# A graph network on one core: unbounded gathers in the second propagation, and three groups' scatters moved from the degrees to the node run

## The chip, the cores and the metric

The kernel runs on one core of a Trainium2 chip. The metric is the device time of one execution in microseconds (us). TensorE is called PE here, VectorE DVE, ScalarE ACT, GpSimd POOL and SyncE SP. A name with q behind it (SPq, ACTq, POOLq) is that engine's sequencer, which issues the DMAs.

## The reference

Four graph layers, each with a residual, work on 100000 nodes of 64 features and 50000 edges `(src, dst)`, which are sorted by `dst`. Only the first matters here. It is a Chebyshev convolution of order 3 with an attention layer behind it:

```python
h = jnp.maximum(_layernorm(x, axis=-1), 0.0)
...
deg = jax.ops.segment_sum(edge_attr, src, num_segments=n)
dinv = jnp.where(deg > 0, 1.0 / jnp.sqrt(jnp.where(deg > 0, deg, 1.0)), 0.0)
w = -(dinv[src] * edge_attr * dinv[dst])

def prop(h):
    return jax.ops.segment_sum(w[:, None] * h[src], dst, num_segments=n)
Tx1 = prop(Tx0)
...
Tx2 = 2.0 * prop(Tx1) - Tx0
```

`Tx1` of a node that is the `dst` of no edge is zero. The edges whose `src` is such a node therefore contribute nothing to the second `prop`.

## The kernel before

The edges lie in 49 groups of 1024 (8 slots of 128 partitions; `EP` = 50176 with padding), the nodes in 98 groups of 1024. The program is a row of stages, each a function with one block of code for each engine; a barrier stands between two stages. Inside a stage each engine runs a software pipeline of its own over the groups (`ring_loop`: every part of a group's work has a lag in steps and a place inside the step), and semaphores tie the engines together. The stages around the change:

- **Degrees** (`degrees`, 0 to 461 us). PE adds up the nodes' degrees as products of one-hot matrices; ACT and DVE build these. At the end DVE makes the factors `dinv` and SP stores them. Beside that POOL writes each edge's place into a table `d_pos` by its final id: one indirect DMA for 128 edges, eight for a group (`scatter_places`, L948). The first `PLACED_EARLY` = 40 groups are done here (L730, 320 DMAs), and POOL then waits for their landing (L731).
- **Node run** (`lone_nodes`, 461 to 1172 us). All 98 node groups are normalized and taken through the layer as if they had no edge. POOL scatters the other nine groups' places (L990, 72 DMAs), waits until all 16 columns of `d_xt` are written, and gathers the destination rows of the 49 edge groups (`gather_kept`, L1173, 8 indirect DMAs a group, 8 buffers). ACT issues these 16 column copies (L1110), one in each of its first 16 steps; every element is a packet of 4 bytes. SP's order is written out step by step: in step `s` it loads `x` of group `s` (L1002); loads the tails `d_dinv` and `d_pos` of group `s - TAIL_LATE` (L1008, L1009; the first of them waits for all scatters); stores the rows `d_ext` of group `s - EXT_LATE`, five steps later (L1013); stores `d_h` and `d_x` of group `s - 7` (L1018, L1022); and stores the gathered rows of edge group `e` at step `xd_turn(e)` (L1027). ACT writes the body of an `ext` row (L1127) early and its tail (L1132) at the lag of the tails, into a ring of 24 buffers.

```python
late = [[] for _ in range(TAIL_LATE - 2)]
ring_loop(act, NODE_GROUPS, [begin, columns], [scale], [base, tables], [mean], *late, [tails], lead=EXT_RING + 2,
          ring=EXT_RING)
```

- **First propagation** (1172 to 1703 us). For each edge group SP loads the source ids `near` and the group's `d_xd`, POOL gathers the source rows of `d_ext` (`gather_rows`, L1165, 8 indirect DMAs, 66 columns), DVE weighs them (`p_msg`, L1265), PE transposes them, DVE adds up along the edges (`run_sums`, a scan), and SP stores the running sums to `d_sums1`. From the last two columns of the gathered row DVE also makes `ls`, the row at which the source's sums lie: below `EP` where that node has incoming edges, at `EP` or beyond where it has none. A test `beyond` (L1260) on `ls` gives `ls2`. SP stores `ls` and `ls2`.
- **Second propagation** (1703 to 2256 us). SP loads `ls` as ids, and POOL gathers rows of `d_sums1` (65 columns) with a bound of `EP - 1`: an id beyond it moves nothing. What is not moved has to be zero already, so DVE clears each buffer `got` behind its use (L1406) and POOL waits for that. DVE weighs the rows (`p_msg`, L1402), PE transposes them (L1437), DVE scans, PE multiplies (L1446, L411, L1457), and so on.

The rest of the program (2256 to 5535 us) isn't touched.

Of the kernel before, what the change touches and what calls it, by code (L numbers as in the profile page):

```python
# [31 lines left out]
P = 128  # L32
# [25 lines left out]
HOT_RING = 16  # L58
HOT_PARTS = ((0, 96), (96, 96), (192, 64), (256, 64), (320, 72))
PRODUCT_PARTS = ((0, 208), (208, 64), (272, 120))  # L60
PLACED_EARLY = 40
PLACED_LATE = GROUPS - PLACED_EARLY
COLUMN_PARTS = 16
WIDE = 2 * S
NODE_RING = 8
H_LATE, X1_LATE = 7, 7
TAIL_LATE = 18
EXT_LATE = TAIL_LATE + 5
EXT_RING = 24


def xd_turn(e):

    return 22 + 17 * (e + 1) // 10


def of_slot(r, n):
# [304 lines left out]
def group_rows(a):  # L382
    return a.rearrange("(g p s) c -> g p s c", p=P, s=S)
# [74 lines left out]
def build(nc, A, out):  # L458
    ctx = ExitStack()
    with ctx:  # L460
# [14 lines left out]
        D = Bufs()  # L475
        D.hs = dram("d_hs", (EP, C))
        D.xt, D.xd = dram("d_xt", (NP_, C + 1)), dram("d_xd", (EP, C + 1))
        D.sums1 = dram("d_sums1", (EP, C + 1))
        D.h, D.x1 = (dram("d_" + name, (EP + NP_, C)) for name in ("h", "x1"))
        D.x23 = dram("d_x23", (2 * EP + NP_, C))  # L480
        D.hd, D.x1d, D.x2d, D.x3d = D.h[0:EP], D.x1[0:EP], D.x23[0:EP], D.x23[EP + NP_:2 * EP + NP_]
        D.h_lone, D.x1_lone, D.x2_lone = (a[EP:EP + NP_] for a in (D.h, D.x1, D.x23))
        D.ext = dram("d_ext", (NP_, C + 2))
        D.dinv, D.pos = dram("d_dinv", (NP_, 1)), dram("d_pos", (NP_, 1))
        D.ls, D.ls2 = (dram("d_" + name, (GROUPS, P, S), I32) for name in ("ls", "ls2"))
# [692 lines left out]
def first_propagation(nc, A, sem, W, D, bank):  # L1178

    ctx = ExitStack()  # L1180
    with ctx:
# [4 lines left out]
        near, ls, ls2 = (t("p1_" + n, [P, RING, S], I32) for n in ("near", "ls", "ls2"))  # L1186
# [4 lines left out]
        pd = t("p1_pd", [C, RING, G_ROWS])  # L1191
        norm = NormTwice(sem, t, "p1_n", bank(6))
        names = ("msg_done", "yd_done", "msg_t", "yd_t", "yf_done", "pd_mm", "back", "evacuated", "carry", "weighed",
                 "placed", "beyond", "wd_done", "placed2")
        m = {n: sem("p1_" + n) for n in names}
        inn, x_in, landed, st, ls_st = ([sem(f"p1_{n}{r}") for r in range(RING)] for n in (
            "in", "x_in", "got", "st", "ls_st"))
        with nc.Block() as block:
            @block.sync
            def _(sp):  # L1200
                for r in range(RING):
                    sp.sem_inc(st[r], 32)
                    sp.sem_inc(ls_st[r], 32)

                def load(i, r, g):
                    sp.wait_ge(m["msg_done"], g + 1)
                    sp.dma_start(near[:, r], A["src_rows"][g]).then_inc(inn[r], 16)
                    sp.wait_ge(m["yd_done"], g + 1)
                    sp.dma_start(xd[:, r], group_rows(D.xd)[g]).then_inc(x_in[r], 16)

                def store_places(i, r, g):
                    sp.wait_ge(m["placed2"], g + 1)
                    sp.dma_start(D.ls[g], ls[:, r]).then_inc(ls_st[r], 16)
                    sp.dma_start(D.ls2[g], ls2[:, r]).then_inc(ls_st[r], 16)

                def store(i, r, g):
                    sp.wait_ge(m["evacuated"], g * 2 + 2)
                    sp.dma_start(group_cols(D.pd)[g], pd[:, r]).then_inc(st[r], 16)
                    sp.dma_start(group_rows(D.sums1)[g], g1[:, r]).then_inc(st[r], 16)
                ring_loop(sp, GROUPS, [load], [], [store_places], [], [store])  # L1220
                for r in range(RING):
                    sp.wait_ge(st[r], 32 * (of_slot(r, GROUPS) + 1))
                    sp.wait_ge(ls_st[r], 32 * (of_slot(r, GROUPS) + 1))

            @block.gpsimd
            def _(pool):
                def gather(i, r, g):
                    hold(pool, inn[r], i * 16 + 16)
                    gather_rows(nc, pool, D.ext, near[:, r], got[:, r], landed[r])
                ring_loop(pool, GROUPS, [gather])  # L1230

            @block.vector
            def _(dve):
                dve.sem_inc(m["yd_done"], RING)
                dve.sem_inc(m["msg_done"], RING)
                nc.vector.memset(sums[:, 1, G_ROWS - 1:G_ROWS], 0.0).then_inc(m["carry"], 1)

                def a(i, r, g):
                    dve.wait_ge(x_in[r], i * 16 + 16)
                    yield from norm.centre(nc, dve, g, xd[:, r, :, 0:C])  # L1240
                    yield 3
                    nc.vector.scalar_tensor_tensor(out=wd[:, r % 2], in0=xd[:, r, :, C], scalar=-1.0, in1=of_group(W.ewE, g),
                                                   op0=ALU.mult, op1=ALU.mult).then_inc(m["wd_done"], 1)
                    yield from norm.scale(nc, dve, g)
                    if not (isinstance(g, int) and g == 0):
                        dve.wait_ge(m["yd_t"], g)
                    nc.vector.tensor_tensor(yd[:], norm.y, spread(norm.gain), ALU.mult).then_inc(m["yd_done"], 1)

                def messages(i, r, g):
                    yield 3  # L1250
                    w = of_group(W.wE, g)
                    dve.wait_ge(landed[r], i * 128 + 128)
                    dve.wait_ge(ls_st[r], i * 32 + 32)
                    dve.wait_ge(m["wd_done"], g + 1)
                    nc.vector.tensor_tensor(w, got[:, r, :, C], wd[:, r % 2], ALU.mult).then_inc(m["weighed"], 1)
                    nc.vector.tensor_tensor(ls[:, r], got[:, r, :, C + 1], of_group(W.loneE, g), ALU.min
                                            ).then_inc(m["placed"], 1)
                    yield 6
                    dve.wait_ge(m["placed"], g + 1)
                    nc.vector.tensor_scalar(beyond[:], ls[:, r], EP, EP + NP_, ALU.is_lt, ALU.mult).then_inc(m["beyond"], 1)  # L1260
                    dve.wait_ge(m["weighed"], g + 1)
                    if not (isinstance(g, int) and g == 0):
                        dve.wait_ge(m["msg_t"], g)
                    nc.vector.tensor_scalar(msg[:, :, C], w, 1.0, None, ALU.mult)
                    nc.vector.tensor_tensor(msg[:, :, 0:C], got[:, r, :, 0:C], spread(w), ALU.mult).then_inc(m["msg_done"], 1)  # L1265
                    dve.wait_ge(m["beyond"], g + 1)
                    nc.vector.tensor_tensor(ls2[:, r], ls[:, r], beyond[:], ALU.add).then_inc(m["placed2"], 1)

                def scan(i, r, g):
                    yield 4  # L1270
                    dve.wait_ge(m["msg_t"], g + 1)
                    if not (isinstance(g, int) and g < 2):
                        dve.wait_ge(m["back"], g - 1)
                    dve.wait_ge(m["carry"], g + 1)
                    run_sums(nc, W, g, r % 2, bank(4, 2)[0:C + 1], sums, m)
                ring_loop(dve, GROUPS, [a, messages], [scan])
# [65 lines left out]
def second_propagation(nc, A, sem, W, D, bank):  # L1342

    ctx = ExitStack()
    with ctx:
# [7 lines left out]
        names = ("msg_done", "zeroed", "msg_t", "carry", "mm", "pre_done", "slanted", "h_done", "back", "att_mm", "evacuated",  # L1353
                 "pd_in0", "pd_in1")
        m = {n: sem("p2_" + n) for n in names}
        pd_in = (m["pd_in0"], m["pd_in1"])
# [1 line left out]
        with nc.Block() as block:  # L1358
            @block.sync
            def _(sp):  # L1360
# [2 lines left out]

                def load(i, r, g):
                    sp.wait_ge(m["msg_done"], g + 1)
                    sp.dma_start(near[:, r], D.ls[g]).then_inc(inn[r], 16)

                def load_later(i, r, g):
                    sp.wait_ge(m["pre_done"], g + 1)
# [10 lines left out]
            @block.gpsimd  # L1380
            def _(pool):
                def gather(i, r, g):
                    hold(pool, inn[r], i * 16 + 16)
                    hold(pool, m["zeroed"], g + 1)
                    gather_rows(nc, pool, D.sums1, near[:, r], got[:, r], landed[r], EP - 1)
                ring_loop(pool, GROUPS, [gather])

            @block.vector
            def _(dve):
                dve.sem_inc(m["msg_done"], RING)  # L1390
                dve.sem_inc(m["pre_done"], 2)
                for r in range(RING):
                    nc.vector.memset(got[:, r], 0.0).then_inc(m["zeroed"], 1)
                nc.vector.memset(sums[:, 1, G_ROWS - 1:G_ROWS], 0.0).then_inc(m["carry"], 1)

                def messages(i, r, g):
                    yield 4
                    dve.wait_ge(landed[r], i * 128 + 128)
                    if not (isinstance(g, int) and g < 2):
                        dve.wait_ge(m["msg_t"], g - 1)  # L1400
                    w = W.wE[:, bass.ds(g, 1)].rearrange("p a s -> p (a s)")
                    nc.vector.tensor_tensor(msg[:, r % 2], got[:, r], spread(w, C + 1), ALU.mult  # L1402
                                            ).then_inc(m["msg_done"], 1)
# [1210 lines left out]
```

## Time and profile before

| | |
|---|---|
| median of 3 runs | 5541.77 us (5536.04 to 5545.48) |
| the profiled execution | 5537.43 us, its span 5535.3 us |
| busy share of the span: PE, DVE, ACT, POOL | 64%, 73%, 50%, 66% |
| mean granted clock of TensorE | 0.78 |
| mean DMA traffic | 108 GB/s |

No engine is busy all the time: each stage has its own limit, so the shares over the whole span tell little. The rows further down are cut by stage. Times in them are counted from the span's start. "Issue" as the end of an idle time means that the engine waited for nothing that the profile shows; the 0.30 us between two of POOL's indirect DMAs are of that kind.

### The profile page before, as it was taken

The numbers are of one execution on the slowest core, as the hardware profiler recorded it, in microseconds if no ns is written. First come the engines' busy times: TensorE is split into PE (matmuls) and PEld (weight loads), VectorE is DVE, ScalarE is ACT, GpSimd is POOL, SyncE is SP. The second block draws the span as 40 slices with busy tenths as digits, with TensorE's granted clock in tenths as the row PEclk, the third lists the DMA queues.
The fourth block names the chain that finished last, engine by engine and source line by source line (L and its number), as shares of the span: only waits on it lengthen the run. The fifth ranks groups of instructions, "written<-read, shape, count | busy, mean of one in ns | idle before, by whom it ended". The sixth has DMA issues, their size and how long they took to land. (4 is left out here: it accounts for less than half of the span.)

```text
span 5535.3 us, 72269 instructions
## 1 busy us (share of the span) xinstructions
PE 3564.5 (64%) x15275; PEld 1835.2 (33%) x15275; DVE 4044.6 (73%) x6567; ACT 2757.9 (50%) x6379; POOL 3627.5 (66%) x3647
## 2 busy tenths in 40 slices
PE   8992788847776999677728867777455545661110
PEld 5551555523332333244414433333222212221000
DVE  8873698857774555699869969999555569996442
ACT  6662677733331222476629966666322247772221
POOL 7777277757775777577713347665377767765777
PEclk9996999978785555699959989999666668885555
DMA  8549977754442222466514433333344423322221
GB/s 99 74 62 43 109 232 232 230 146 108 103 108 55 62 62 62 134 212 195 183 60 138 135 98 84 84 84 84 91 129 132 125 68 77 77 68 67 70 74 48
DMA packets 535690, 595.56 MB, mean 108 GB/s; under 512 B 297571, under 2 KB 312041, under 8 KB 533948
## 3 DMA queue, kind: packets, MB, share of 16 engines
q1 hardware_dynamic: 319036, 473.91, 29.2%
q0 software_dynamic: 112896, 91.81, 9.2%
q10 hardware_dynamic: 103648, 28.71, 6.6%
q8 instruction: 29, 0.48, 0.0%
q14 instruction: 81, 0.66, 0.0%
HBM read 354.69 MB, written 303.31 MB: 119 GB/s over the span
## 5 line engine op out<-in xcount | busy, mean ns | idle before, releaser
L1165 POOL DMA_INDIRECT l_got<-d_x,l_near x1176 | 1139.2, 969 | 562.1 <-issue 373.7
L1173 POOL DMA_INDIRECT ln_xd<-d_xt,idsE x392 | 370.1, 944 | 208.3 <-issue 119.2
L2480 POOL DMA_INDIRECT out<-fi_res,fi_near x392 | 381.1, 972 | 181.0 <-issue 118.5
L1165 POOL DMA_INDIRECT p_got<-d_sums,p_near x392 | 399.5, 1019 | 151.7 <-issue 150.5
L948 POOL DMA_INDIRECT d_pos<-placeE,finE x392 | 401.9, 1025 | 146.4 <-issue 135.6
L1165 POOL DMA_INDIRECT p_got<-d_h,p_near x392 | 384.8, 982 | 156.5 <-issue 117.2
L1165 POOL DMA_INDIRECT p_got<-d_ext,p_near x392 | 378.5, 965 | 162.8 <-issue 117.1
L892 PE MATMUL ps<-hot_lo,hot_w 128*128 128x392 bf16 x2352 | 391.9, 330 | 15.6 <-ACT hot_w L930 15.6
L930 ACT ACTIVATE hot_w<-hot_hi,vals 128x128 bf16<-128x128 bf16 x784 | 267.9, 393 | 126.2 <-DVE hot_lo L787 114.5
L411 PE MATMUL ps<-ident,fi_sums 64*128 64x64 f32 x392 | 53.1, 314 | 424.8 <-DVE fi_sums L1338 424.8
L1338 DVE TENSOR_TENSOR_SCAN p_sums<-same,p_sums,ps 65x1024 f32<-65x1024 f32 (+1 forms) x98 | 229.5, 2342 | 95.1 <-PE ps L1437 90.9
L892 PEld LDWEIGHTS ps<-hot_lo,hot_w 128*128 128x128 bf16 x2352 | 230.3, 98 | 176.8 <-issue 17.7
L404 PE MATMUL ps<-ident,l_hn 128*128 128x128 f32 x588 | 111.2, 321 | 230.8 <-DVE l_hn L2259 205.2
L418 PE MATMUL ps<-l_df,l3ab 128*64 128x512 f32 x196 | 165.4, 998 | 128.4 <-DVE l_neg L2380 128.4
L1338 DVE TENSOR_TENSOR_SCAN l_sums<-same,l_sums,ps 64x1024 f32<-64x1024 f32 (+1 forms) x98 | 228.7, 2334 | 5.7
L2568 ACT ACTIVATE ps<-fi_hh,fi_sc 64x1024 f32<-64x1024 f32 x49 | 59.0, 1205 | 336.8 <-DMA fi_hh<-d_hh 332.6
L1468 ACT ACTIVATE p_slant<-ps 64x1024 f32<-64x1024 f32 x49 | 49.8, 1017 | 348.6 <-DVE ps L1420 348.6
L1988 PE MATMUL ps<-at_pf,gatw 128*64 128x512 f32 x392 | 178.2, 597 | 54.3 <-DVE at_sums L1338 53.9
L1912 POOL TENSOR_TENSOR at_wide<-at_wide,at_own 128x512 f32<-128x512 f32 x49 | 70.3, 1434 | 215.9 <-DVE at_wide L1932 214.7
L2547 DVE TENSOR_TENSOR fi_res<-fi_xd,ps 128x512 f32<-128x512 f32 x49 | 33.6, 685 | 241.9 <-POOLq L2487 241.9
L418 PE MATMUL ps<-l_hf,l2w 128*64 128x512 f32 x196 | 173.5, 1041 | 46.5 <-ACT l_hf L2303 46.5
L240 ACT ACTIVATE l_hn<-l_s_xc,l_s_rstd 128x64 f32<-128x64 f32 x784 | 196.3, 333 | 0.3 <-DVE l_s_rstd L226 0.3
(388 smaller groups left out, 10934.3 us busy)
## 6 DMA issues: line engine op xcount, KB each, us to landing
l_xd<-d_x SPq DMA_DIRECT2D x147, 256.0 KB
d_ext<-ln_ext SPq DMA_DIRECT2D x98, 264.0 KB, 2.2
d_xt<-in_x_wide ACTq DMA_DIRECT2D x49, 520.0 KB
ln_x<-in_x SPq DMA_DIRECT2D x98, 256.0 KB
d_h<-ln_hb SPq DMA_DIRECT2D x98, 256.0 KB, 3.0
d_x<-ln_x SPq DMA_DIRECT2D x98, 256.0 KB
lb_x<-d_x SPq DMA_DIRECT2D x49, 512.0 KB
d_x<-lb_x SPq DMA_DIRECT2D x49, 512.0 KB
```

The lines of the kernel that those rows point to most:

```text
L240: last = nc.scalar.activation(out[:, n], self.xc[:, r % 2, n], func, scale=self.rstd[:, n:n + 1])
L404: last = nc.tensor.transpose(out[:, P * n:P * n + P], flat[:, P * n:P * n + P], W.ident[:])
L418: last = nc.tensor.matmul(out[:, HALF * h:HALF * h + HALF], weights[:, h], paired, start=True, stop=True)
L892: last = nc.tensor.matmul(bank(h)[:, 0:TABLE_HALF], hot_w[:, r, k], hot_lo[:, r, TABLE_HALF * h:TABLE_HALF * h + TABLE_HALF], start=False, ...
L930: last = nc.scalar.activation(hot_w[:, r, k], hot_hi[:, r], ACT.Copy, scale=vt[:, k:k + 1])
L948: nc.gpsimd.indirect_dma_start(out=D.pos, out_offset=bass.IndirectOffsetOnAxis(ap=W.finE[:, g, q:q + 1], axis=0), in_=W.placeE[:, g, q:q + ...
L1165: nc.gpsimd.indirect_dma_start(out=out[:, q], out_offset=None, in_=source, in_offset=bass.IndirectOffsetOnAxis(ap=ids[:, q:q + 1], axis=0) ...
L1173: nc.gpsimd.indirect_dma_start(out=out[:, q], out_offset=None, in_=source, in_offset=bass.IndirectOffsetOnAxis(ap=ids[:, g, q:q + 1], axis ...
L1338: return nc.vector.tensor_tensor_scan(sums[:, par], same, messages, sums[:, 1 - par, G_ROWS - 1:G_ROWS], ALU.mult, ALU.add).then_inc(m["ca ...
L1912: nc.gpsimd.tensor_tensor(wide[:, r % 2, 0:JOINED], wide[:, r % 2, 0:JOINED], own[:, r % 2, 0:JOINED], ALU.add).then_inc(m["joined"], 1)
L1988: last = nc.tensor.matmul(bank(4, 2)[0:C, HALF * h:HALF * h + HALF], W.gatw[:, q], pf[:, h, q], start=q == 0, stop=q == 1)
L2480: nc.gpsimd.indirect_dma_start(out=out, out_offset=bass.IndirectOffsetOnAxis(ap=near[:, r, q:q + 1], axis=0), in_=res[:, r, q], in_offset= ...
```

## The change

- `PLACED_EARLY` goes from 40 to 37: three groups' scatters (24 DMAs) move from the degrees to the node run. There `TAIL_LATE` goes from 18 to 20, so that the tails and, with `EXT_LATE`, the stores of `d_ext` come two steps later, and `xd_turn` by four.
- In the first propagation `d_sums1` gets 128 rows more, and SP stores zeros there before its first load. A second set of ids, `lz`, is the minimum of `ls` and `EP + p` on partition `p` (one more DVE instruction for a group), and SP stores it as a third array.
- In the second propagation SP loads `lz`, and POOL gathers without a bound: an id at `EP` or beyond reads its partition's row of zeros. The clearing of `got` and the wait for it are gone.

```diff
-PLACED_EARLY = 40
+PLACED_EARLY = 37
...
-TAIL_LATE = 18
+TAIL_LATE = 20
...
-    return 22 + 17 * (e + 1) // 10
+    return 26 + 17 * (e + 1) // 10
...
-        D.sums1 = dram("d_sums1", (EP, C + 1))
+        D.sums1 = dram("d_sums1", (EP + P, C + 1))
...
@@ first propagation, SP @@
+                sp.wait_ge(m["nothing"], 1)
+                sp.dma_start(D.sums1[EP:EP + P], nothing[:]).then_inc(m["empty_st"], 16)
...
                     sp.dma_start(D.ls2[g], ls2[:, r]).then_inc(ls_st[r], 16)
+                    sp.dma_start(D.lz[g], lz[:, r]).then_inc(ls_st[r], 16)
...
@@ first propagation, POOL @@
+                nc.gpsimd.iota(empty_i[:], pattern=[[1, 1]], base=EP, channel_multiplier=1).then_inc(m["iota"], 1)
...
@@ first propagation, DVE @@
+                nc.vector.memset(nothing[:], 0.0).then_inc(m["nothing"], 1)
+                dve.wait_ge(m["iota"], 1)
+                nc.vector.tensor_copy(empty[:], empty_i[:]).then_inc(m["empty"], 1)
...
                     nc.vector.tensor_tensor(msg[:, :, 0:C], got[:, r, :, 0:C], spread(w), ALU.mult).then_inc(m["msg_done"], 1)
+                    dve.wait_ge(m["empty"], 1)
+                    nc.vector.tensor_scalar(lz[:, r], ls[:, r], empty[:], None, ALU.min)
...
@@ second propagation, SP @@
-                    sp.dma_start(near[:, r], D.ls[g]).then_inc(inn[r], 16)
+                    sp.dma_start(near[:, r], D.lz[g]).then_inc(inn[r], 16)
...
@@ second propagation, POOL @@
-                    hold(pool, m["zeroed"], g + 1)
-                    gather_rows(nc, pool, D.sums1, near[:, r], got[:, r], landed[r], EP - 1)
+                    gather_rows(nc, pool, D.sums1, near[:, r], got[:, r], landed[r])
...
@@ second propagation, DVE @@
-                for r in range(RING):
-                    nc.vector.memset(got[:, r], 0.0).then_inc(m["zeroed"], 1)
...
-                    yield 5
-                    dve.wait_ge(m["msg_done"], g + RING + 1)
-                    nc.vector.memset(got[:, r], 0.0).then_inc(m["zeroed"], 1)
```

POOL's order from the end of its preparation in the degrees to its first gathers of the node run, as a difference:

```order
 L723 MEMSET ident 128x128
 L725 AFFINE_SELECT ident<-ident 128x128
-L948 DMA d_pos<-placeE,finE 100352x1 x320
+L948 DMA d_pos<-placeE,finE 100352x1 x296
 L686 UNCONDITIONAL_BRANCH
 L547 ISA
 L988 UNCONDITIONAL_BRANCH
-L948 DMA d_pos<-placeE,finE 100352x1 x72
+L948 DMA d_pos<-placeE,finE 100352x1 x96
 L1173 DMA ln_xd<-d_xt,idsE 128x65 x392
```

The 24 scatters stand behind the stage's end (L547) now, ahead of all gathers of `d_xt`.

SP's order at the end of the node run, from the last store of `d_x` on, before:

```order
L1022 DMA d_x<-ln_x 128x512
L1008 DMA ln_tail<-d_dinv 128x8
L1009 DMA ln_tail<-d_pos 128x8
L1013 DMA d_ext<-ln_ext 128x528
L1027 DMA d_xd<-ln_xd 128x520
L1008 DMA ln_tail<-d_dinv 128x8
L1009 DMA ln_tail<-d_pos 128x8
L1013 DMA d_ext<-ln_ext 128x528
```

and after the change:

```order
L1022 DMA d_x<-ln_x 128x512
L1027 DMA d_xd<-ln_xd 128x520
L1008 DMA ln_tail<-d_dinv 128x8
L1009 DMA ln_tail<-d_pos 128x8
L1013 DMA d_ext<-ln_ext 128x528
L1027 DMA d_xd<-ln_xd 128x520
L1008 DMA ln_tail<-d_dinv 128x8
L1009 DMA ln_tail<-d_pos 128x8
L1013 DMA d_ext<-ln_ext 128x528
L1008 DMA ln_tail<-d_dinv 128x8
L1009 DMA ln_tail<-d_pos 128x8
L1013 DMA d_ext<-ln_ext 128x528
```

Both go on in threes (two tails, one `ext`) and end with six stores of `ext` in a row. Behind that last store of `d_x` stand 11 groups' tails, 16 stores of `ext` and one of `d_xd` before, and 13, 18 and four after.

One round of DVE in the second propagation's loop, before:

```order
L1402 TENSOR_TENSOR p_msg<-p_got,wE 128x520
L1405 REGISTER_ALU
L1406 MEMSET p_got 128x520
L1338 ISA
L1338 SCALAR_TENSOR_TENSOR p_sums<-same,p_sums,ps 65x1024
L1420 TENSOR_TENSOR ps<-ps,p_pd 64x1024
L1422 REGISTER_ALU
L1426 SCALAR_TENSOR_TENSOR p_hf<-p_slant,ps 64x1024
```

and after, where the lines count some more (L1412 is L1402 of before, L1351 is L1338):

```order
L1412 TENSOR_TENSOR p_msg<-p_got,wE 128x520
L1351 ISA
L1351 SCALAR_TENSOR_TENSOR p_sums<-same,p_sums,ps 65x1024
L1427 TENSOR_TENSOR ps<-ps,p_pd 64x1024
L1429 REGISTER_ALU
L1433 SCALAR_TENSOR_TENSOR p_hf<-p_slant,ps 64x1024
```

Only the clearing and its register's step are gone; the rest keeps its order.

## Rows read from the trace of the kernel before

**Rows 1.** Stages: length; busy PE, PEld, DVE, ACT, POOL (count); clock; DMA share; GB/s.

```profile
461.00:1172.00 711.00, 518.64 (x2842) 354.85 (x2842) 526.73 (x980) 467.27 (x980) 440.05 (x464) 0.92 0.89 185
1172.00:1703.00 531.00, 365.51 (x1372) 177.08 (x1372) 386.36 (x836) 190.46 (x343) 378.47 (x392) 0.79 0.44 100
1703.00:2256.00 553.00, 494.73 (x1176) 176.91 (x1176) 290.89 (x249) 123.16 (x147) 399.46 (x392) 0.50 0.24 58
```

**Rows 2.** POOL's scatters (L948), 420 to 452: ns min/median/max, first and last start.

```profile
L948 POOL DMA_INDIRECT d_pos<-placeE,finE x24: 971/972/1573, 420.1 to 450.1; - x24
```

**Rows 3.** POOL's timeline, 449 to 463: start, us, instruction, idle before, releaser.

```profile
461.85 0.97 POOL L948 DMA_INDIRECT d_pos<-placeE,finE  x1 [10.79 <-POOLq L548]
```

**Rows 4.** DMA traffic 423 to 433, in 40 slices.

```profile
GB/s 1 0 0 0 13 376 426 414 364 14 1 0 2 0 0 0 0 2 0 0 0 0 1 1 0 0 0 1 1 0 0 0 1 2 0 0 0 0 2 0
```

**Rows 5.** Column copies' queue, 461 to 553, then 553 to 642: packets, MB, share.

```profile
q10 hardware_dynamic: 44759, 0.18, 96.6%
...
q10 hardware_dynamic: 55849, 0.22, 92.4%
```

**Rows 6.** ACT's column issues (L1110), from 473 to 556, then 556 to 640.

```profile
L1110 ACTq DMA_DIRECT2D d_xt<-dinv_table x6: 4045/8595/13548, 473.7 to 540.7; - x6
...
L1110 ACTq DMA_DIRECT2D d_xt<-dinv_table x8: 1382/5086/7676, 556.8 to 622.4; - x8
```

**Rows 7.** POOL's gathers of the node run (L1173), and what they waited for.

```profile
L1173 POOL DMA_INDIRECT ln_xd<-d_xt,idsE x392: 940/944/980, 642.6 to 1130.9; - x196
...
  DMA d_xt<-dinv_table: 89.1, 1
```

**Rows 8.** SP's timeline at the end of the node run.

```profile
1158.59 0.43 SPq L1013 DMA_DIRECT2D d_ext<-ln_ext  x1
...
1160.03 0.43 SPq L1013 DMA_DIRECT2D d_ext<-ln_ext  x1
```

**Rows 9.** SP's, then ACT's timeline: ext's first store, the ring's first reuse.

```profile
684.02 0.43 SPq L1013 DMA_DIRECT2D d_ext<-ln_ext  x1
...
697.62 0.62 ACT L1127 ACTIVATE ln_ext<-ln_a_four 128x512 f32<-128x512 f32 x1
```

**Rows 10.** The page's DMA issues: KB of one, us to landing.

```profile
d_ext<-ln_ext SPq DMA_DIRECT2D x98, 264.0 KB, 2.2
```

**Rows 11.** POOL's gathers of both propagations (L1165); DVE's bound test (L1260).

```profile
L1165 POOL DMA_INDIRECT p_got<-d_ext,p_near x392: 940/944/1410, 1175.5 to 1672.2; - x196
...
L1165 POOL DMA_INDIRECT p_got<-d_sums,p_near x392: 992/997/2036, 1705.7 to 2223.3; - x196
...
L1260 DVE TENSOR_SCALAR p_beyond<-p_ls x49: 148/241/378, 1188.5 to 1680.7; 128x8 f32<-128x8 int32 x49
```

**Rows 12.** PE's timeline: first transposes of group 0, then 45 to 48.

```profile
1718.16 1.09 PE L1437 MATMUL ps<-ident,p_msg 128*65 128x128 f32 x4 [22.71 <-DVE p_msg L1402]
...
2196.51 1.94 PE L1437 MATMUL ps<-ident,p_msg 128*65 128x128 f32 x8 [0.90 <-DVE p_msg L1402]
...
2206.86 1.94 PE L1437 MATMUL ps<-ident,p_msg 128*65 128x128 f32 x8 [0.25 <-issue]
...
2217.10 1.94 PE L1437 MATMUL ps<-ident,p_msg 128*65 128x128 f32 x8
...
2228.23 0.66 PE L1437 MATMUL ps<-ident,p_msg 128*65 128x128 f32 x2 [1.03 <-DVE p_msg L1402]
```

**Rows 13.** Waits from 1706 to 2240: us in total, times, longest.

```profile
PE ps L1437 <- DVE p_msg L1402: 54.0, 16, 22.7
DVE p_msg L1402 <- DMA p_got<-d_sums,p_near: 32.5, 16, 13.0
```

**Rows 14.** POOL's queue, 1176 to 1674, then 1706 to 2225: packets, MB, share.

```profile
q0 software_dynamic: 12512, 13.24, 16.8%
...
q0 software_dynamic: 12512, 4.72, 7.0%
```

**Rows 15.** The same queue, 1674.9 to 1676.5.

```profile
q0 software_dynamic: 32, 0.03, 10.0%
```

More of the change, by code:

```diff
@@ L484, in build @@
         D.dinv, D.pos = dram("d_dinv", (NP_, 1)), dram("d_pos", (NP_, 1))
-        D.ls, D.ls2 = (dram("d_" + name, (GROUPS, P, S), I32) for name in ("ls", "ls2"))
+        D.ls, D.ls2, D.lz = (dram("d_" + name, (GROUPS, P, S), I32) for name in ("ls", "ls2", "lz"))
         D.same = dram("d_same", (1, EP), U8)
@@ L1185, in first_propagation @@
         turned = bank(0, 2).rearrange("p (h n) -> p h n", h=2)[:, :, 0:S // 2 * (C + 1)]
-        near, ls, ls2 = (t("p1_" + n, [P, RING, S], I32) for n in ("near", "ls", "ls2"))
+        near, ls, ls2, lz = (t("p1_" + n, [P, RING, S], I32) for n in ("near", "ls", "ls2", "lz"))
+        empty_i, empty = t("p1_empty_i", [P, 1], I32), t("p1_empty", [P, 1])
+        nothing = t("p1_nothing", [P, C + 1])
         beyond, wd = t("p1_beyond", [P, S]), t("p1_wd", [P, 2, S])
@@ L1193, in first_propagation @@
         names = ("msg_done", "yd_done", "msg_t", "yd_t", "yf_done", "pd_mm", "back", "evacuated", "carry", "weighed",
-                 "placed", "beyond", "wd_done", "placed2")
+                 "placed", "beyond", "wd_done", "placed2", "iota", "nothing", "empty", "empty_st")
         m = {n: sem("p1_" + n) for n in names}
@@ L1202, in _ @@
                     sp.sem_inc(st[r], 32)
-                    sp.sem_inc(ls_st[r], 32)
+                    sp.sem_inc(ls_st[r], 48)
+                sp.wait_ge(m["nothing"], 1)
+                sp.dma_start(D.sums1[EP:EP + P], nothing[:]).then_inc(m["empty_st"], 16)
                 def load(i, r, g):
@@ L1218, in store @@
                     sp.dma_start(group_cols(D.pd)[g], pd[:, r]).then_inc(st[r], 16)
-                    sp.dma_start(group_rows(D.sums1)[g], g1[:, r]).then_inc(st[r], 16)
+                    sp.dma_start(group_rows(D.sums1[0:EP])[g], g1[:, r]).then_inc(st[r], 16)
                 ring_loop(sp, GROUPS, [load], [], [store_places], [], [store])
@@ L1222, in _ @@
                     sp.wait_ge(st[r], 32 * (of_slot(r, GROUPS) + 1))
-                    sp.wait_ge(ls_st[r], 32 * (of_slot(r, GROUPS) + 1))
+                    sp.wait_ge(ls_st[r], 48 * (of_slot(r, GROUPS) + 1))
+                sp.wait_ge(m["empty_st"], 16)
             @block.gpsimd
             def _(pool):
+                nc.gpsimd.iota(empty_i[:], pattern=[[1, 1]], base=EP, channel_multiplier=1).then_inc(m["iota"], 1)
                 def gather(i, r, g):
@@ L1252, in messages @@
                     dve.wait_ge(landed[r], i * 128 + 128)
-                    dve.wait_ge(ls_st[r], i * 32 + 32)
+                    dve.wait_ge(ls_st[r], i * 48 + 48)
                     dve.wait_ge(m["wd_done"], g + 1)
@@ L1352, in second_propagation @@
         att = t("p2_att", [2 * HEADS, RING, G_ROWS])
-        names = ("msg_done", "zeroed", "msg_t", "carry", "mm", "pre_done", "slanted", "h_done", "back", "att_mm", "evacuated",
+        names = ("msg_done", "msg_t", "carry", "mm", "pre_done", "slanted", "h_done", "back", "att_mm", "evacuated",
                  "pd_in0", "pd_in1")
```

## The prediction

> **What bounds the kernel now.** I read the table of stages first, then in each stage the engine that starts late or ends last.
>
> The **degrees** stage ends on POOL. Its last 24 scatters run from 420.1 to 450.1 [rows 2], and the next stage's first one starts at 461.85, after 10.79 us without work [rows 3]. Everything else is over long before: the last transfer of another engine, SP's store of the factors, is the burst in the 6th to 9th slice of a quarter us behind 423, gone by 425.5 [rows 4]. So POOL's last 24 us are bare.
>
> The **node run** [rows 1] starts with DMAs: ACT issues one of 16 column copies (4-byte elements) in each of its first 16 steps, POOL's gathers wait 89.1 us for them and start at 642.6 [rows 7], and the queue of the copies fills 96.6% and 92.4% of the DMA engines [rows 5]. It ends on SP, which issues one DMA behind the other, a step of three in 1160.03 - 1158.59 = 1.44 us [rows 8].
>
> The **first propagation** is POOL's: 378.47 us of gathers [rows 1] plus 0.30 us between two, 392 × (0.944 + 0.30) = 488 of its 531 us [rows 1, 11].
>
> The **second propagation** is set by POOL and PE together: TensorE is busy 494.73 of 553 us at a clock of 0.50, its lower level of 1.2 GHz [rows 1], yet waits 16 times for the messages and DVE 16 times for a gather [rows 13]. From its first transposes at 1718.16 to the 49th group's at 2228.23 it takes 510.07 / 48 = 10.63 us for a group; where no data is late, two groups take 2217.10 - 2196.51 = 20.59, that is 10.30 each [rows 12]. POOL needs 8 × (0.997 + 0.30) = 10.38 plus (399.46 - 392 × 0.997) / 49 = 0.18 for gathers that last longer [rows 1, 11]: 10.56. So POOL is just slower than PE, and sets the pace.
>
> **The change, part by part.**
>
> *24 scatters leave the degrees.* They are the 24 of [rows 2]: one each 1.25 to 1.3 us. The 296th then ends where the 297th starts now, 0.3 us before 420.1. POOL ends 451.1 - 419.8 = 31.3 us earlier; I take **-31.2**. The 10.79 us behind it stay and reach to 430.6; SP's store, gone at 425.5, is the next to be late. Bounds: -31.3, and -25.5 if as long a stretch has to follow on SP's traffic (425.5 + 10.8 = 436.3).
>
> *They land in the node run*, whose scatters then take 96 × 1.277 = 122.6 us instead of 92. On POOL that hides under the 89.1 us of waiting. But the copies run beside them: 44759 packets in 92 us, 486 a us, with scatters; 55849 in 89 us, 627.5 a us, without [rows 5]. All copies are 100608 packets. With scatters for 122.6 us: 122.6 × 486.5 = 59640, and 40968 more at 627.5 take 65.3, together 187.9 against 181 now: **+6.9**. Since ACT issues the copies between its own work and the gathers start behind them, that delay moves the whole run. Bounds: 0, if the slower 92 us are slow for other reasons (the first loads fall there), and 10.5, three copies at the difference of the medians, 8.595 - 5.086 [rows 6].
>
> *Later tails, stores of ext and of xd.* A step takes some 6 us (711 us for 98 + 23). The first store of xd goes from step 23 to 27, so it comes some 44 us behind its gather rather than 20 (that ends at 652.6 [rows 7]; step 25 is at 684.02 [rows 9]), and POOL needs the buffer again after 8 groups of 10 us, 80. The ring of 24 ext buffers is tighter: ext's first store goes from step 23 to 25, which is issued at 684.02 today, and ACT overwrites that buffer at 697.62 [rows 9]; 13.6 us for a landing of 2.2 [rows 10]. So nothing in the steady part. In the drain SP alone is the path: behind the last store of d_x stand two more groups of tails (four issues), two more of ext and three more of xd, as the order shows. 9 × 0.48 = **+4.3**. Bounds 0 (if the DVE end before it moves, not SP) and 5.
>
> *Zero rows.* SP waits for a memset and issues one store ahead of the first index load; an issue is 0.43 us [rows 8]: **+0.4**; IOTA and the cast run while that load lands. The third store of each group (4 KB) goes to SP, which is not the bound in this stage. Bounds 0 and 2.
>
> *The minimum.* 49 DVE instructions of the shape of the bound test beside it, 128x8 with one tensor input: 0.148 to 0.378, median 0.241 us [rows 11]. They stand behind the message's product, and DVE is busy 386 of 531 us [rows 1], so on DVE they hide. If that cover were gone they would cost 49 × 0.241 = 11.8. POOL is the path, so what counts is whether they stretch gathers. All of its longer gathers together make 378.47 - 392 × 0.944 = 8.4 us now, and each that I looked at lies beside the message's product, which reads two tensors, none beside the bound test. I take **+0.5**, bounds 0 and 8.4 (that many again). The Trainium skill, "SBUF — State Buffer", section "Who interferes with whom", speaks against the change here: a tensor_scalar can take the port pair that VectorE shares with GpSimd, and holds GpSimd up for its whole length. By that rule the term would be 11.8; no row here shows it, as the bound test is itself such an instruction and the gathers beside it are not longer.
>
> *Gathers without a bound.* Beside one with a bound (0.997) stands the same function without, from rows of 66 columns: 0.944 [rows 11]. POOL's need falls to 8 × (0.944 + 0.30) + 0.18 = 10.13, below PE's 10.30. PE becomes the pace: 48 × (10.63 - 10.30) = **-15.7**. That needs PE to find its data each time; if the longer gathers (8.6 us in all) still come through as waits, it is -7.1. If PE gave way too, POOL alone without longer gathers would make 48 × (10.63 - 9.95) = -32.6, the other end. The 53 memsets (and the wait for them) were off the path: DVE is busy 290.89 of 553 us, and POOL waits for them in no row.
>
> *More rows to read.* A bounded gather skips ids past the table; now all 1024 of a group are read. The queue moved 13.24 MB in 12512 packets in the first propagation and 4.72 MB in as many in the second [rows 14]: 36% of the ids are in the table, some 654 of each group go to the zero rows. At the first propagation's price the queue's share goes from 7.0 to 16.8% of a stage that has 0.24 in all [rows 1, 14]: hidden.
>
> **Sum:** -31.2 + 6.9 + 4.3 + 0.4 + 0.5 - 15.7 = -34.8 us. It was made on the profiled execution (5537.43, span 5535.3), 4.3 us under the median of 5541.77, which takes the same step: **5507**. A difference under 0.2%, 11 us, is one that these runs can't tell from none.
>
> **The rivals.**
>
> *The copies suffer more (0.08).* Three more copies beside scatters could each take a whole 8.6 us that now pass later at no cost: +25.8 in place of 6.9, 5526. For it: ACT's issue of a copy took up to 13.5 us beside scatters and 7.7 behind them [rows 6]. Against: the queue is never idle in either stretch [rows 5].
>
> *The minimum locks POOL (0.05).* 49 × 0.241 to 0.378: 11.8 to 18.5 in place of 0.5, 5518 to 5525.
>
> *The gather is no shorter without the bound (0.04).* Then the change doesn't do what its last part says; the second propagation stays at 10.63, 5523. Against: the unbounded gathers of the node run and of the first propagation, with rows of 65 and of 66 columns, both have 0.944 [rows 7, 11].
>
> *TensorE's clock rises (0.05).* In the second propagation the clock is granted at 0.50 while PE is busy 89%; the node run has 0.92 with 73% [rows 1]. Were a PE without waits granted 2.4 GHz, POOL would stay the bound at 10.13 to 9.95 us: -24 to -32.6 in place of -15.7, 5490 to 5499. The Trainium skill, "TensorE: Matmul & The Clock Gate", Part 1, says that the throttled state is the default and that activity releases it, which would make this likely. The trace disagrees so far: from 2196.51 to 2217.10 PE waits once, 0.25 us, and its round is no shorter at the end of that [rows 12].
>
> *The zero rows are a hot spot, and the change is slower (0.03).* All 654 of a group fall on one block of 33 KB, the same 128 rows each time. If that block serves one row after the other, the second propagation takes 654 times that price for a group. From 17 ns a row it would be 11.25 us, which eats up the rest of the gain and 11 us more; at 25 ns it is 16.35 us a group, +290 in all, about 5800. Against it: the last gather of the first propagation, whose 128 padded ids all name one row, put 32 packets through in 10.0% of 1.6 us × 16 engines [rows 15], 0.080 us for a packet, less than the 16.8% × 498 × 16 / 12512 = 0.107 of random rows [rows 14].
>
> **How the numbers follow.** The forecast has 0.73, the five rivals 0.25, the rest 0.02 is a stall I don't see. The range: the low end takes no harm to the copies and, in the second propagation, the middle of -15.7 and -32.6 (-31.2 + 0 + 4.3 + 0.4 + 0 - 24 = -50.5, 5491); the high end takes 10.5 for the copies, 8.4 for longer gathers and -7.1 at the end (-14.7, 5527), and so holds three of the rivals (5518 to 5526): **5491 to 5527**. Of the cases only the hot spot and the unseen stall end above 5530.7 or near it: faster 0.92, same 0.04, slower 0.04.
>
> **What would show it.** The node run should begin at 430.7 rather than 461.9; the first gather of d_xt at some 618 (642.6 - 31.2 + 6.9); SP's last issue 4 us later within its run than now. In the second propagation the gathers' median should be 0.944, POOL should wait for index loads (its ring is full), PE should start a group every 10.30 us, and 49 times 10.3 plus the fill make about 537 us. It is wrong if the node run is over 20 us longer, if gathers of the first propagation have a mean above 0.98, if those of the second stay at 0.997 or their landing, not PE, releases DVE, or if the zero rows' packets take far over 0.107 us.

## The result and the profile after

| | before | after |
|---|---|---|
| median of 5 runs | 5541.77 us | 5507.6 us |
| lowest to highest | 5536.04 to 5550.69 | 5503.73 to 5516.88 |
| the profiled execution | 5537.43 us, span 5535.3 | 5507.24 us, span 5505.5 |

The ratio of the runs is 0.9942, with a 95% interval of 0.9931 to 0.9954: the change is faster by 34.2 us between the medians. Forecast were 34.8. In the third set of experiments one run of the kernel before (5797.87 us) and one of e11_tail12 (5594.69 us) had a lower granted clock (0.65 and 0.715) and are left out of what follows.

The stages of the changed kernel, with the columns of [rows 1] (length; busy PE, PEld, DVE, ACT, POOL; clock; DMA share; GB/s):

```profile
429.00:1143.00 714.00, 521.18 (x2842) 358.38 (x2842) 526.78 (x982) 467.35 (x980) 463.43 (x489) 0.91 0.89 184
1143.00:1677.00 534.00, 364.00 (x1372) 175.11 (x1372) 391.61 (x886) 190.37 (x343) 380.82 (x392) 0.79 0.44 100
1677.00:2217.00 540.00, 494.75 (x1176) 176.89 (x1176) 264.48 (x196) 123.13 (x147) 385.51 (x392) 0.50 0.29 75
```

The node run is 3 us longer than in [rows 1], the first propagation 3, the second 13 shorter; the degrees end 32 earlier. Three lines tell how. POOL's timeline around the first scatter of the node run (against [rows 3]):

```profile
429.57 0.97 POOL L948 DMA_INDIRECT d_pos<-placeE,finE  x1 [8.76 <-POOLq L548]
```

and POOL's gathers (L1165) of both propagations, with minimum, median and maximum in ns (against [rows 11]):

```profile
L1165 POOL DMA_INDIRECT p_got<-d_ext,p_near x392: 940/944/1467, 1146.5 to 1645.5; - x196
L1165 POOL DMA_INDIRECT p_got<-d_sums,p_near x392: 938/944/1458, 1680.0 to 2183.7; - x196
```

In the second propagation the median fell from 0.997 to 0.944. There PE now runs almost without a stop from the fourth group on; its timeline at the first transposes (L1444 is L1437 of before) of groups 0 and 3 and of the last ones (44, 45 and 48), against [rows 12]:

```profile
1692.21 1.94 PE L1444 MATMUL ps<-ident,p_msg 128*65 128x128 f32 x8 [22.85 <-DVE p_msg L1412]
...
1724.43 1.94 PE L1444 MATMUL ps<-ident,p_msg 128*65 128x128 f32 x8
...
2147.19 1.94 PE L1444 MATMUL ps<-ident,p_msg 128*65 128x128 f32 x8 [0.30 <-issue]
...
2157.43 1.94 PE L1444 MATMUL ps<-ident,p_msg 128*65 128x128 f32 x8
...
2188.77 1.94 PE L1444 MATMUL ps<-ident,p_msg 128*65 128x128 f32 x8 [0.66 <-DVE p_msg L1412]
```

(2188.77 - 1692.21) / 48 = 10.345 us a group, where it was 10.63. Without the filling, in which PE still waits 8.52 and 6.13 us for the messages of the second and third group, it is (2157.43 - 1724.43) / 42 = 10.31. The waits of that stretch (1680 to 2201; total, times, longest), against [rows 13]:

```profile
PE ps L1444 <- DVE p_msg L1412: 38.2, 4, 22.8
POOL p_got L1165 <- DMA p_near<-d_lz: 37.6, 14, 33.6
DVE p_msg L1412 <- DMA p_got<-d_sums,p_near: 22.5, 4, 15.2
```

PE waits for messages 4 times instead of 16: for the first three groups and, 0.66 us, for the last. The pace has gone over to PE. POOL shows no wait for that: 33.6 of its 37.6 us stand ahead of the first group, and the other 13 are the usual 0.30 us between two gathers. Its gathers got longer instead. Beyond 392 × 0.944 they take 385.51 - 370.05 = 15.5 us, where it was 8.6 beyond 392 × 0.997, and each of the 47 gathers over 1.05 us lies beside DVE's product for a message. How this keeps POOL at PE's pace is not shown.

### The profile page after: what moved, and what is told of

Same layout as the page of the kernel before. It is cut to its first block and busy times, and to the rows that moved or that the text cites. A ratio compares the mean times of both kernels' runs of the same rounds, so it can differ in the third digit from the quotient of the medians.

```text
span 5505.5 us, 71826 instructions
## 1 busy us (share of the span) xinstructions
PE 3585.0 (65%) x15275; PEld 1844.6 (34%) x15275; DVE 4024.9 (73%) x6565; ACT 2758.7 (50%) x6379; POOL 3616.6 (66%) x3648
## 5 line engine op out<-in xcount | busy, mean ns | idle before, releaser
L1165 POOL DMA_INDIRECT l_got<-d_x,l_near x1176 | 1137.4, 967 | 564.6 <-issue 349.4
L948 POOL DMA_INDIRECT d_pos<-placeE,finE x392 | 401.3, 1024 | 145.3 <-issue 136.5
L1165 POOL DMA_INDIRECT p_got<-d_h,p_near x392 | 388.9, 992 | 156.6 <-issue 117.9
L1173 POOL DMA_INDIRECT ln_xd<-d_xt,idsE x392 | 370.0, 944 | 179.8 <-issue 119.2
L1165 POOL DMA_INDIRECT p_got<-d_sums,p_near x392 | 385.5, 983 | 152.8 <-issue 115.2
L1165 POOL DMA_INDIRECT p_got<-d_ext,p_near x392 | 380.8, 971 | 122.8 <-issue 113.1
L1351 DVE TENSOR_TENSOR_SCAN p_sums<-same,p_sums,ps 65x1024 f32<-65x1024 f32 (+1 forms) x98 | 229.6, 2342 | 126.0 <-PE ps L1444 122.2
L1351 DVE TENSOR_TENSOR_SCAN l_sums<-same,l_sums,ps 64x1024 f32<-64x1024 f32 (+1 forms) x98 | 228.7, 2334 | 5.7
L2554 DVE TENSOR_TENSOR fi_res<-fi_xd,ps 128x512 f32<-128x512 f32 x49 | 33.6, 685 | 241.8 <-POOLq L2494 241.8
```

The costliest lines, as they stand in the source:

```text
L948: nc.gpsimd.indirect_dma_start(out=D.pos, out_offset=bass.IndirectOffsetOnAxis(ap=W.finE[:, g, q:q + 1], axis=0), in_=W.placeE[:, g, q:q + ...
L1165: nc.gpsimd.indirect_dma_start(out=out[:, q], out_offset=None, in_=source, in_offset=bass.IndirectOffsetOnAxis(ap=ids[:, q:q + 1], axis=0) ...
L1173: nc.gpsimd.indirect_dma_start(out=out[:, q], out_offset=None, in_=source, in_offset=bass.IndirectOffsetOnAxis(ap=ids[:, g, q:q + 1], axis ...
L1351: return nc.vector.tensor_tensor_scan(sums[:, par], same, messages, sums[:, 1 - par, G_ROWS - 1:G_ROWS], ALU.mult, ALU.add).then_inc(m["ca ...
```

## The experiments

Eleven kernels ran, in three sets; in each set the kernel before ran beside them. Its median was 5544.0, 5569.3 and 5552.8 us, and each set ran on another chip, so totals are compared inside a set, by the ratio, and stages by the traces. Stretches below are read from the traces: "the copies" is from SP's first load of the node run to POOL's first gather of `d_xt`, "the drain" from the end of DVE's last sum to SP's last store of `ext`, and a propagation's stretch is from its first gather's start to its last one's end.

| kernel (scatters in the node run) | the copies | the drain | first propagation | second |
|---|---|---|---|---|
| before (72) | 181.5 | 24.5 | 497.7 | 518.6 |
| the change (96) | 183.6 | 28.9 | 500.0 | 504.7 |
| e1_place (96) | 189.7 | 29.0 | 496.6 | 521.1 |
| e2_prop (72) | 178.1 | 25.1 | 500.0 | 503.7 |
| e3_tail18 (96) | 187.7 | 24.5 | 500.1 | 504.0 |
| e4_tail14 (96) | 185.8 | 18.7 | 498.7 | 504.5 |
| e5_place48 (8) | 181.3 | 29.0 | 499.6 | 504.2 |
| e6_place30 (152) | 239.2 | 28.7 | 498.7 | 504.2 |
| e7_lz5 (96) | 212.8 | 29.2 | 496.9 | 503.5 |
| e8_hot (96) | 222.9 | 30.0 | 501.2 | 502.8 |
| e9_memset (96) | 190.3 | 28.8 | 500.1 | 504.1 |
| e10_bound (96) | 188.0 | 28.8 | 499.7 | 519.9 |
| e11_tail12 (96) | 188.2 | 15.8 | 499.2 | 503.5 |

e1 to e4 are the first set, e5 to e8 the second, e9 to e11 the third.

### Each part alone

**e1_place** is the kernel before with the placement part only.

```diff
-PLACED_EARLY = 40
+PLACED_EARLY = 37
...
-TAIL_LATE = 18
+TAIL_LATE = 20
...
-    return 22 + 17 * (e + 1) // 10
+    return 26 + 17 * (e + 1) // 10
```

> Only the placement part (37 groups early, tails at 20, xd four steps later) in the kernel before; the second propagation keeps its bound and its clearing. By the forecast's terms: -31.2 + 6.9 + 4.3 = -20.0, 5522. Theory from the changed kernel's trace: the copies are not slowed by the scatters (the run up to DVE's last sum was 1.7 us shorter, not 6.9 longer), so -32.3 - 1.7 + 4.4 = -29.6, 5512; first gather of the first propagation about 29 us earlier than before.

Measured: 5523.83 us, a ratio of 0.9961 (0.9946 to 0.9976), 20.2 us under the kernel before beside it. The forecast's terms gave 20.0; the theory made from one pair of traces gave 29.6, which lies at the far end of the interval (13 to 30 us). Its stretch of the copies speaks for the first: 189.7 us, where the pair had shown 183.6.

**e2_prop** is the changed kernel with the old placement.

```diff
-PLACED_EARLY = 37
+PLACED_EARLY = 40
...
-TAIL_LATE = 20
+TAIL_LATE = 18
...
-    return 26 + 17 * (e + 1) // 10
+    return 22 + 17 * (e + 1) // 10
```

> Only the propagation part (zero rows, minimum, no bound), with the placement of before. By the forecast's terms: 0.4 + 0.5 - 15.7 = -14.8, 5527. Theory from the trace: 0.4 + 2.3 (longer gathers in the first propagation) + 1.0 (its end) - 13.0 = -9.3, 5532.5. If nothing in the untouched stages answers to the change, those agree with before within their scatter.

Measured: 5529.86 us, 0.9974 (0.9962 to 0.9987), 14.1 us less. Again the forecast's -14.8 is nearer than the pair's -9.3, but the interval, 7 to 21 us, holds both. The parts add up, 20.2 + 14.1 = 34.3, each known to some 8 us. Its profiled execution began the node run at 468.7 instead of 461.1, with the same program up to there. One scatter of 10.3 us accounts for that; POOL's scatters in this trace, in ns:

```profile
L948 POOL DMA_INDIRECT d_pos<-placeE,finE x392: 966/972/10325, 10.1 to 560.1; - x196
```

### The later tails

**e3_tail18** and **e4_tail14** are the changed kernel with earlier tails and the old steps of xd; **e11_tail12** goes further.

```diff
-TAIL_LATE = 20
+TAIL_LATE = 18
...
-    return 26 + 17 * (e + 1) // 10
+    return 22 + 17 * (e + 1) // 10
```

(14 and 12 in the others.)

> The changed kernel with the tails and xd at their old steps (18; 22), 37 groups early. Theory: SP's issues behind the last sum are the whole price of the later steps, 9 x 0.48 = 4.3 us; the time falls to 5503, and the stretch from DVE's last sum to SP's last store of ext from 28.9 to 24.5. Rival: the later tails are needed, as the 96 scatters end later; then SP waits at step 18 for them, DVE waits for x, and the time is 5507 or more.

> The same with the tails at 14 and the stores of ext at 19. Theory: six steps of tails fewer behind the last sum than in the changed kernel, 18 issues and three of xd, 21 x 0.48 = 10.1 us: 5497.5, the stretch about 18.9. Rival: step 14 comes at about 550 us, the scatters land at about 554; SP waits there with the loads of x behind it, and some 4 us or more come back: 5502 and up.

> The changed kernel with the tails at 12, the stores of ext at 17 and xd at its old steps. Theory: eight steps of tails fewer behind the last sum than at 20, 24 issues and three of xd, 27 x 0.48 = 13.0 us less: 28.9 - 13 = 16 us from the last sum to the last store of ext, ratio to the kernel before some 0.9915. Rival: step 12 comes before the 96 scatters have landed, SP stands with the loads of x behind it, and the stretch up to the last sum grows by 5 us or more; then it is no better than with the tails at 14 (0.992).

Measured: 5501.0 us, 0.9921 (0.9908 to 0.9935); 5497.51, 0.9920 (0.9905 to 0.9935); and in its set 5500.97, 0.9900 (0.9877 to 0.9922). The first two intervals touch that of the change (0.9931 to 0.9954), the third, of another set, lies below it. The drain came as expected to 0.2 us: 28.9, 24.5, 18.7 and 15.8 us with the tails at 20, 18, 14 and 12, where 24.5, 18.9 and 16 were expected. The last store of `ext` (SP's, first and last start) and DVE's last sum in e11_tail12:

```profile
L1013 SPq DMA_DIRECT2D d_ext<-ln_ext x98: 320/430/765, 606.3 to 1129.7; - x98
```

```profile
L1067 DVE TENSOR_TENSOR ln_x<-ln_x,ps x98: 678/680/689, 471.9 to 1113.2; 128x512 f32<-128x512 f32 x98
```

The sum starts at 1113.2 and takes 0.68; the store follows 15.8 us behind its end. In the change the two start at 1137.4 and 1107.7, and the drain is 28.9. The wait that the rivals named did come with the tails at 14 and 12, though not its price. In e11_tail12 the last scatter ended at 551.1, and SP stood from a load of `x` to the first load of a tail (in e4_tail14 from 551.7 to 560.3; with the tails at 18 the scatters were over in time):

```profile
525.32 0.53 SPq L1002 DMA_DIRECT2D ln_x<-in_x  x1
561.86 0.33 SPq L1008 DMA_DIRECT2D ln_tail<-d_dinv  x1
```

But from the first load to the last sum's end the run took 686.0 us, with the tails at 14 685.9, at 18 688.2, at 20 679.6, 683.8 and (in the third set) 690.3 and 688.9. From POOL's first gather of `d_xt` to the last sum's end it is 497.8 us in e11_tail12, and 490 to 501 in all thirteen traces, so no price of SP's wait is seen outside the stretch of the copies. So with 37 groups early the tails need not be later, and e11_tail12 has the lowest ratio here, though its interval overlaps that of e4_tail14.

### The copies

**e5_place48** and **e6_place30** move only the number of groups early.

```diff
-PLACED_EARLY = 37
+PLACED_EARLY = 48
```

(30 in the other.)

> The changed kernel with 48 groups' scatters early, one (8 DMAs, 10 us) in the node run. Theory of the forecast: the copies run at 486 packets a us beside scatters and at 627.5 without, so 10 x 486 + 95700 / 627.5 = 163 us from the node run's first load to POOL's first gather of d_xt (180 with 40 early, 184 to 190 with 37). Rival: the first 92 us are slow for the first loads of x; then it stays near 180. The degrees end 88 x 1.277 = 112 us later than with 37 early, about 541.

> The changed kernel with 30 groups early, 152 scatters (194 us) in the node run. Theory: all copies run beside scatters, 100608 / 486 = 207 us to the first gather of d_xt. Rival: 184 to 190 as with 37. The degrees then end on SP's store, at 427, 1 to 2 us earlier than with 37, and POOL has been done for 70 us. SP waits at step 20 for the scatters, so the whole is slower, 5525 or more.

Measured: 1.0097 (1.0070 to 1.0125) and 0.9969 (0.9951 to 0.9987) of the kernel before. SP's first loads (L1002) start at 546.0 in e5_place48 and at 428.7 in e6_place30. POOL's gathers (L1173; first and last start) of e5_place48:

```profile
L1173 POOL DMA_INDIRECT ln_xd<-d_xt,idsE x392: 940/944/977, 727.3 to 1215.6; - x196
```

and of e6_place30:

```profile
L1173 POOL DMA_INDIRECT ln_xd<-d_xt,idsE x392: 940/944/977, 667.9 to 1156.2; - x196
```

727.3 - 546.0 = 181.3 us with 8 scatters, 667.9 - 428.7 = 239.2 with 152. The numbers expected (163 and 207) were both missed. In this set the copies are slower: 212.8 and 222.9 with 96 scatters, where the other sets have 183.6 to 190.3. The kernel before, too, took 25 us longer here than in the first set. Inside the set the sense is clear: 57.9 us between 8 and 152 scatters, 0.40 for each; the rival, no difference, fell, though its number for 8 scatters, 180, came by the slower set. Between 72 and 96, in the first pair and the first set, it is 179.8 (mean of two) against 186.7 (mean of four): +6.9, 0.29 each. Why the second set's copies are slower was not found; set and chip can't be told apart here.

That the first 92 us are slow for the first loads of `x` is answered by one stretch, 92 to 123 us behind the first load, in which the scatters of before are over and those of the change still run. The copies' queue there, before (553.1 to 584.1) and in the change (520.8 to 551.8):

```profile
q10 hardware_dynamic: 19926, 0.08, 101.5%
...
q10 hardware_dynamic: 15315, 0.06, 97.0%
```

That is 643 and 494 packets a us. In the second set it is 601 without scatters (e5_place48) and 393 to 409 beside them (the other three).

e6_place30 also shows where POOL's lead ends: its last early scatter starts at 349.3, 70 us earlier than with 37 groups, and the node run still begins at 428.7 (428.8 in the change), now on SP's store. SP did not wait for the scatters at step 20, as had been expected: they ended at 638.1, and the first load of a tail came at 662.1. The degrees of e5_place48 ended at 546.0 rather than 541; one of its scatters took 6.0 us.

### The minimum

**e7_lz5** makes the minimum five times.

```diff
+                    for k in range(4):
+                        nc.vector.tensor_scalar(spare[:, k], ls[:, r], empty[:], None, ALU.min)
                     nc.vector.tensor_scalar(lz[:, r], ls[:, r], empty[:], None, ALU.min)
```

> The minimum is made five times for each group. The runs with one minimum took 2.5 us longer from the first to the last gather of the first propagation (499.7 against 497.2). Theory: each one stretches a gather a little, so four more cost 10 us, 510. Theory of the shared port pair held for the whole instruction: 4 x 49 x 0.24 = 47 us, 547. Rival: the 2.5 us came from another alignment of the message's product, and 500 stays.

Measured: 496.9 us in the first propagation, as without any minimum (497.7 and 496.6). The time was 0.9945 (0.9926 to 0.9964) of the kernel before. The rows of the page, with busy us and the mean in ns, in the change:

```profile
L1165 POOL DMA_INDIRECT p_got<-d_ext,p_near x392 | 380.8, 971 | 122.8 <-issue 113.1
```

and in e7_lz5 (378.5 us in the kernel before, 377.4 in e1_place):

```profile
L1165 POOL DMA_INDIRECT p_got<-d_ext,p_near x392 | 377.8, 964 | 122.9 <-issue 113.1
```

The forecast's sentence on the Trainium skill, "SBUF — State Buffer", section "Who interferes with whom", had a tensor_scalar that takes the port pair hold GpSimd for its whole length. By that rule the 196 more instructions, at 221 ns in this trace, would cost an estimated 43 us here; none of it is seen. With one minimum the ten traces have 498.7 to 501.2 us (mean 499.7), without any 496.6 and 497.7, and with five 496.9. So the 2.5 us are no price of the instruction. They are the longer gathers: beyond 392 × 0.944 = 370.0 us the gathers take 10.8 us in the change, 8.5 in the kernel before and 7.8 in e7_lz5, and nearly all of that (9.6, 8.5 and 7.3 us) in gathers that overlap the message's product. How the gathers fall against that product differs, then; that it is another alignment of DVE's round against POOL's, which five instructions shift once more, was not tested.

### Zero rows, clearing and bound

**e8_hot** sends all ids past the table to one row.

```diff
-                    nc.vector.tensor_scalar(lz[:, r], ls[:, r], empty[:], None, ALU.min)
+                    nc.vector.tensor_scalar(lz[:, r], ls[:, r], float(EP), None, ALU.min)
```

> All ids past the table name one row of zeros (the bound itself) instead of one for each partition: some 654 reads of one row for a group. Theory: rows of one place cost no more than others, the second propagation stays at 504 us from first to last gather and the time at 5507. Rival (hot spot): at 17 ns a read the stage takes 11.1 us a group, 545; the time 5548 or more.

Measured: 0.9944 (0.9930 to 0.9957), as the change; the second propagation took 502.8 us. The rival's price fell: the stage doesn't take 654 reads one after the other. But the reads of one row are slower. POOL's queue in 1739 to 2242 of e8_hot:

```profile
q0 software_dynamic: 12499, 13.03, 39.4%
```

That is 0.254 us for a packet, where e7_lz5 in the same set has 14.1% in 504 us, 0.091. The stage hides it: the DMA engines are 57% busy, and PE keeps its steady round of 10.32 us (10.31 in e7_lz5).

**e9_memset** puts the clearing and POOL's wait back, **e10_bound** the bound.

POOL's and DVE's part of the first:

```diff
+                    hold(pool, m["zeroed"], g + 1)
                     gather_rows(nc, pool, D.sums1, near[:, r], got[:, r], landed[r])
...
+                    yield 5
+                    dve.wait_ge(m["msg_done"], g + RING + 1)
+                    nc.vector.memset(got[:, r], 0.0).then_inc(m["zeroed"], 1)
```

SP's and POOL's part of the second:

```diff
-                    sp.dma_start(near[:, r], D.lz[g]).then_inc(inn[r], 16)
+                    sp.dma_start(near[:, r], D.ls[g]).then_inc(inn[r], 16)
...
-                    gather_rows(nc, pool, D.sums1, near[:, r], got[:, r], landed[r])
+                    gather_rows(nc, pool, D.sums1[0:EP], near[:, r], got[:, r], landed[r], EP - 1)
```

> The changed kernel with the clearing of the gather's buffers, and POOL's wait for it, put back; the gathers stay unbounded. Theory: the clearing cost nothing, the bound did; the second propagation stays at 504 us from its first to its last gather, and a group at 10.34. Rival: the clearing and the wait were the cost; it goes back to 519 to 521.

> The other half: the bounded gather is put back, without the clearing in the loop (the first four buffers are cleared once; from then on an id past the table leaves an older row in place, so the second propagation adds other rows than the reference). Theory: 519 to 521 us as before, gathers of 0.997 and a group at 10.6. Rival: without the clearing 504 to 510, as POOL loses no time to it.

Measured: 0.9925 (0.9902 to 0.9949) and 0.9971 (0.9953 to 0.9989); 504.1 and 519.9 us in the second propagation. The gathers of e9_memset:

```profile
L1165 POOL DMA_INDIRECT p_got<-d_sums,p_near x392: 941/947/1452, 1690.5 to 2193.7; - x196
```

and of e10_bound:

```profile
L1165 POOL DMA_INDIRECT p_got<-d_sums,p_near x392: 993/1000/1997, 1687.2 to 2206.2; - x196
```

The bound's 53 ns, 20.8 us over 392 gathers, are the whole of the gain. Of them 15.8 come through, and 5.0 go into longer gathers, which grow from 8.7 to 13.7 us; the clearing was free.

## Why the prediction was right

**The degrees: -31.2 forecast, -32.3 measured** (first load of the node run at 428.8 after 461.1). The scatters gave 30.2 of it (POOL's last ends at 420.8, where 419.8 was forecast). The other 2.0 are the stretch behind the last scatter, which did not stay at 10.79 us; it is 8.76, since POOL's DRAIN at the stage's end took 5.8 us instead of 7.7 (3.7 behind e5_place48's 384 scatters, 1.2 behind e6_place30's 240; why is open). That POOL was alone at the end is shown by e6_place30, and that little more can be had too: there SP's store ends the stage, and begins the node run hardly sooner.

**The copies: +6.9 forecast, +2.1 in the first pair of traces, +6.9 in the mean of the pair and the first set.** The step stands, though the pair alone seemed to refute it: the copies move at 494 packets a us beside scatters and at 643 without, in the same stretch of the run, and from the first load to the last sum's end the same six traces have 676.9 us with 72 scatters and 684.4 with 96. The stretch varies by 3 to 6 us between executions of one placement, so a term of that size can't be read from two traces, and that the mean agrees to a tenth is luck. The rival of +25.8 fell in the first and third sets; the second has no trace with 72 scatters.

**The drain: +4.3 forecast, 28.9 - 24.5 = +4.4 measured**, and e3_tail18, e4_tail14 and e11_tail12 lie on the same line.

**The zero rows' store: +0.4, measured 1143.55 - 1143.15 = 0.40** from its issue (L1207) to that of the first index load (L1211) in SP's timeline.

**The minimum: +0.5 forecast, some +2.5 measured.** The most mis-sized term; it lay inside its bounds (0 to 8.4), and its cause is not the instruction's length (e7_lz5): the time stands in gathers beside the message's product, and why there are more or longer ones with one minimum is open.

**The bound: -15.7 forecast**; -13.9 in the pair by the gathers (-13.5 by PE's transposes, 510.07 to 496.56), -15.8 between e10_bound and e9_memset. PE's steady round is 10.31 us, as the 10.30 read from two rounds had it; the 10.345 over all groups counts the filling, which the forecast left out, and is 2 us of the pair's difference. Before itself lies low in it, 518.6 where the two other bounded runs have 519.9 and 521.1. One sign did not come: POOL was to wait for index loads, and no wait holds it to PE's pace, but longer gathers fill its time (15.5 us in the change, 8.6 before): it takes not 10.13 us a group but (385.51 + 391 × 0.305) / 49 = 10.30. That PE sets the pace rests on its own rows: it waits for no message from the fourth group to the 48th. The rows' reading was cheaper than priced: POOL's queue in 1680 to 2185,

```profile
q0 software_dynamic: 12512, 13.04, 12.1%
```

that is 12.1% × 505 × 16 / 12512 = 0.078 us for a packet, as the padded gather of [rows 15] had it (0.080), not 0.107. In the hot spot's rival 654 times 17 ns are 11.1 us, not 11.25; and a single row, which it did not have, does slow the reads (e8_hot).

**The clock did not rise.** PE between 1730 and 2180 of the change, columns as above:

```profile
1730.00:2180.00 450.00, 440.66 (x1053) 158.12 (x1054) 234.82 (x176) 110.46 (x132) 343.35 (x351) 0.50 0.30 80
```

PE is busy 98% of 450 us and the granted clock stays at its lower level, 0.50. The rule cited for that rival, that activity releases the throttle (the Trainium skill, "TensorE: Matmul & The Clock Gate", Part 1), is not borne out by this stage.

**The sum.** The profiled pair differs by 29.8 us, the medians by 34.2. Of the first, 8.9 us were given back behind POOL's first gather of the stage after the second propagation, in code that the change doesn't touch: 3274.5 us from there to the end before, 3283.4 after. The eleven other traces have 3276.9 to 3286.5 there, with the same code, so this is scatter, and the trace of before is the shortest of all. That the forecast lies within 0.6 us of the difference of the medians is luck in part: the interval reaches from 25 to 38 us, and the degrees came out 1.1 us better and the minimum 2 worse than forecast.

## What to carry to other kernels

Price each stage by the engine that ends it, and add the terms; here six terms gave 34.8 us against 34.2 between the medians, while a single pair of traces was off by 5 us in one term and by 2 in two others. Work that is moved onto an idle engine can still slow another engine's transfers beside it, so count the neighbours of a step and not only its own engine. When a step is made later in a written-out order, look at what is left to issue after the last useful result: a step of the tails was worth 1.45 us (24.5 to 15.8 over six steps), and earlier ones gave that back. An engine that keeps another's pace need not show a wait for it: here POOL's gathers grew longer.

## What was not expected of the hardware

- An indirect gather with a bound takes 0.053 us longer on POOL than one without (0.997 against 0.944; 1.000 against 0.947 in the third set).
- Reading one row of DRAM 654 times in a group of 1024 made a packet 2.8 times as long as reading 128 rows (0.254 against 0.091 us), and left the time of the stage as it was, since PE sets it (502.8 against 503.5 to 504.7 us).
- Once in a while one scatter of the degrees lasts 6 to 21 us instead of 0.97, in the traces of e2_prop, e5_place48, e8_hot and e3_tail18. With POOL at the end of that stage, the node run starts later by about as much (in e3_tail18, whose longest took 14.1, at 443.7 rather than 428.8).
- The same placement gives copies of 184 to 190 us in two sets and 213 to 223 in another, each set on a chip of its own.
